# The first two blocks of a retention and FFN kernel: another order of v, q, k and g, x and weights loaded in one paced run, and tiles 4 to 7 transposed on TensorE

## The reference

```python
xn = _layernorm(x)
q1, k1 = apply_rotary(xn @ Wq, xn @ Wk)        # 4 heads of 256
v = xn @ Wv                                    # 4 heads of 512
...
    attn = einsum('bhid,bhjd->bhij', qb, kb) * D
    o_intra = einsum('bhij,bhjd->bhid', attn, vb)
    o_inter = einsum('bhid,bhde->bhie', qb * cross_q, S)
    S_new = gC * S + einsum('bhjd,bhje->bhde', kb * cross_k, vb)
...
s = (rmsnorm(o) * silu(xn @ Wg)) @ Wo
g = _silu(ffn(xn))                             # down(silu(gate) * up)
x = x + s * g
```

## Time and profile before

| | before |
|---|---|
| time, 3 runs | median 2100.38 us, 2098.61 to 2416.41 |
| profiled execution | 2097.79 us |
| its span on the slowest core | 2095.9 us (cores: 2090.8 to 2095.9) |
| TensorE busy | 2037.7 us, 97% of the span |
| VectorE, ScalarE, POOL busy | 697.3, 489.5, 360.2 us |
| granted TensorE clock, mean | 0.992 |
| chain that ended last | PE 94%, DMA 3%, DVE 1%, issue 1%, SPq 1% |

### The profile page before, as it was taken

How to read it: one execution, slowest core, us unless ns; L and a number is a source line. 1 busy time by engine, 2 the same in 40 slices (tenths; PEclk the granted TensorE clock), 3 DMA queues, 4 the chain that set the end, 5 groups by cost and what they waited for, 6 DMA issues and landing times.

```text
span 2095.9 us, 28365 instructions; the slowest of 8 cores (2090.8 to 2095.9 us)
## 1 busy us (share of the span) xinstructions
PE 2037.7 (97%) x9484; PEld 937.6 (45%) x9676; DVE 697.3 (33%) x1156; ACT 489.5 (23%) x880; POOL 360.2 (17%) x996
## 2 busy tenths in 40 slices
PE   5789999999999999999999999999999999999998
PEld 3334444444444444444444444444444444444443
DVE  4444445442232231132234454545311211211211
ACT  2333343442101101101013443343210110110110
POOL 1134444444100000000103333333300000000000
PEclk9899999999999999999999999999999999999999
DMA  7666888769645545545733334534772352452432
GB/s 166 134 93 108 113 122 138 140 122 221 188 115 176 146 109 179 155 118 170 140 75 58 64 65 73 86 67 88 169 216 71 121 171 71 140 151 71 152 90 70
DMA packets 221501, 257.80 MB, mean 123 GB/s; under 512 B 140336, under 2 KB 157872, under 8 KB 221360
## 3 DMA queue, kind: packets, MB, share of 16 engines
q1 hardware_dynamic: 191408, 201.44, 35.0%
q0 software_dynamic: 29952, 54.54, 19.0%
HBM read 244.39 MB, written 46.14 MB: 139 GB/s over the span
## 4 chain that ended last, share of the span: by engine, by line
PE 94%; DMA 3%; DVE 1%; issue 1%; SPq 1%; ACT 0%; POOL 0%; DVEq 0%; ACTq 0%; POOLq 0%
PE R L381 61%; PE U L697 16%; PE OA L716 11%; PE U L492 2%; PE OA L524 2%; PE OA L519 1%; DMA xa<-x 1%; DMA xnT<-xn 1%; PE R L471 1%; DMA wvA<-wv 1%; DMA ktok<-kT 0%; SPq L202 0%; SPq L198 0%; ACT xn L335 0%; DVE st L296 0%
## 5 line engine op out<-in xcount | busy, mean ns | idle before, releaser
L381 PE MATMUL R<-xnT,wgu 128*128 128x512 bf16 x3010 | 663.3, 379 | 3.3
L381 PEld LDWEIGHTS R<-xnT,wgu 128*128 128x128 bf16 x3072 | 300.4, 98 | 361.0
L697 PE MATMUL U<-wd_sb,hT 128*128 128x512 bf16 x1504 | 334.7, 379 | 1.6
L669 DVE TENSOR_TENSOR hT<-sg,R 128x512 bf16<-128x512 bf16 x192 | 131.9, 688 | 492.1 <-PE R L381 482.7
L660 ACT ACTIVATE sg<-R 128x512 bf16<-128x512 f32 x192 | 114.6, 597 | 568.3 <-PE R L381 545.9
L697 PEld LDWEIGHTS U<-wd_sb,hT 128*128 128x128 bf16 x1536 | 150.3, 98 | 181.2
L716 PE MATMUL OA<-wo_sb,ogl 128*128 128x512 bf16 x1006 | 225.3, 379 | 1.0
L504 DVE SCALAR_TENSOR_TENSOR S<-S,U 128x1024 bf16<-128x1024 bf16 x112 | 136.7, 1220 | 203.7 <-PE U L492 199.4
L724 DVE TENSOR_TENSOR g<-g,OA 128x1024 f32<-128x1024 f32 x32 | 39.1, 1222 | 430.8 <-PE OA L716 430.8
L716 PEld LDWEIGHTS OA<-wo_sb,ogl 128*128 128x128 bf16 x1024 | 100.2, 98 | 120.8
L708 ACT ACTIVATE g<-U 128x1024 f32<-128x1024 f32 x32 | 32.7, 1023 | 481.8 <-PE U L697 465.5
(11 more groups left out here) (87 smaller groups left out, 1639.6 us busy)
## 6 DMA issues: line engine op xcount, KB each, us to landing
wgu<-wgu_bf SPq DMA_DIRECT2D x192, 512.0 KB, 4.4
og_sp<-og SPq DMA_DIRECT2D x128, 128.0 KB, 4.0
ox<-x SPq DMA_DIRECT2D x32, 512.0 KB, 5.7
out<-ox SPq DMA_DIRECT2D x32, 512.0 KB, 3.1
wd_sb<-fdw POOLq DMA_DIRECT2D x48, 256.0 KB, 7.7
xa<-x SPq DMA_DIRECT2D x16, 512.0 KB, 9.5
xl<-x SPq DMA_DIRECT2D x16, 512.0 KB, 5.3
wgu_bf<-fgw POOLq DMA_DIRECT2D x24, 256.0 KB, 6.1
```

What stands on the lines that cost most here:

```text
L381: ins = e.matmul(ring[r][:, :], l, m, start=(k == 0), stop=(k == KC - 1))
L669: t_ev = DVE.do(lambda e: e.tensor_mul(out=hT[:, m * 512:(m + 1) * 512], in0=sg[:, g0:g0 + 512], in1=ring[r][:, :]), sDVE)
L697: ins = e.matmul(U[:, n * 512:(n + 1) * 512], hT[:, k * 512 + tt * 128:k * 512 + (tt + 1) * 128], wd_sb[:, k * D + n * 512:k * D + (n + 1) ...
```

## The change

Sequence 0 gets its groups in another order: for the first two blocks v of block 0, q and k of block 0, v of block 1, g of block 0, q and k of block 1, g of block 1. Blocks 2 and 3 keep theirs (two v, q and k, two v, g), and so do all others. `ret.slot(p - 12)` is unchanged and now goes by the running number p. Tiles 4 to 7 are transposed on TensorE, behind p = 7 (tiles 4 and 5) and p = 9 (6 and 7), with their applies and the chain of 6 and 7 placed among the groups of block 0. SP loads xa 0 to 7 and the first two rope tables in one run without a wait; POOL starts two pieces of wvA without a wait, the other two when xa 0 is there, wqA and wkA when xa 3 is, wgA when xa 5 is. xa 12 to 15 are loaded behind p = 9. The chain of tiles 8 to 11 moves forward to p = 16, that of 12 to 15 back by one group, and the applies from n = 7 and 9 to n = 8 and 10. The second `warm` has 24 matmuls and not 44.

```diff
-    def order(s, bi):
-        if s == 0 and bi < 2:
-            return (4, 5, 6, 7, 0, 1, 2, 3, 8, 9, 10, 11)
...
+    def order(s):
+        qk, v, g = (0, 1, 2, 3), (4, 5, 6, 7), (8, 9, 10, 11)
+        if s:
+            return [(bi, x) for bi in range(16) for x in qk + v + g]
+        first = [(0, v), (0, qk), (1, v), (0, g), (1, qk), (1, g)]
...
-    xa_load(2)
-    xa_load(3)
-    POOL.wait(xa_tok[0])
-    for a_ in w_pieces(0, 0):
+    for t in (2, 3, 4, 5):
+        xa_load(t)
+    cs_load(0)
+    for t in (6, 7):
+        xa_load(t)
+    cs_load(1)
+    for n, a_ in enumerate(w_pieces(0, 0)):
+        if n in (2, 4, 8):
+            POOL.wait(xa_tok[{2: 0, 4: 3, 8: 5}[n]])
         w_load(*a_)
...
-    warm(44)
-    ln0_pair(2, True)
-    SP.wait(w_tok[(0, 0, 2)])
-    cs_load(0)
-    for t in range(4, 8):
-        xa_load(t)
-    for t in (4, 6):
-        ln0_pair(t, False)
-        ln0_trans(t, ln_tok[t])
-        ln0_trans(t + 1, ln_tok[t + 1])
-    cs_load(1)
+    warm(24)
+    ln0_pair(2)
+    apply0(2, False)
+    apply0(3, True)
+    ln0_pair(4)
...
+    def ln0_step(p):
+        if p < 2:
+            ln_trans_pe(p + 2, ln_tok[p + 2])
+        elif p == 3:
+            apply0(4, True)
+            apply0(5, True)
+        elif p == 5:
+            ln0_pair(6)
+            apply0(6, False)
+        elif p == 7:
+            apply0(7, True)
+            ln_trans_pe(4, ln_tok[4])
+            ln_trans_pe(5, ln_tok[5])
+        elif p == 9:
+            ln_trans_pe(6, ln_tok[6])
+            ln_trans_pe(7, ln_tok[7])
+            for t in range(12, 16):
+                xa_load(t)
+        elif 12 <= p < 40:
+            t, n = 8 + 4 * (p // 12 - 1), p % 12
+            if p < 24 and n < 4 or p >= 24 and n in (0, 1, 4, 6):
+                ln0_stats(t + (n if p < 24 else (0, 1, 4, 6).index(n)))
+            elif n == (4 if p < 24 else 7):
+                ln_tok["c"] = ln0_chain(0, 4)
+            elif n in (8, 10):
+                for u in (t + n - 8, t + n - 7):
+                    apply0(u, True)
+                    ln0_trans(u, ln_tok[u])
```

More of the change, by code:

```diff
@@ L356, in ln_trans_pe @@
         t_pe = PE.do(tr, sPE)
-        xn0_free[t] = t_pe
+        xn0_free[t % 8] = t_pe
         ACT.wait(t_pe)
@@ L739, in warm, with ln0_pair, apply0 @@
             PE.do(lambda e: e.matmul(ring[3][:, 0:256], idm_sb[:, 0:128], idm_sb[:, :], start=True, stop=True))
-    def order(s, bi):
-        if s == 0 and bi < 2:
-            return (4, 5, 6, 7, 0, 1, 2, 3, 8, 9, 10, 11)
-        if s == 0 and bi < 4:
-            return (4, 5, 0, 1, 2, 3, 6, 7, 8, 9, 10, 11)
-        return range(12)
+    def order(s):
[3 more added lines that the diff above has]
+        first = [(0, v), (0, qk), (1, v), (0, g), (1, qk), (1, g)]
+        for bi in (2, 3):
+            first += [(bi, v[:2]), (bi, qk), (bi, v[2:]), (bi, g)]
+        first += [(bi, qk + v + g) for bi in range(4, 16)]
+        return [(bi, x) for bi, xs in first for x in xs]
     ln_tok = {}
-    def ln0_pair(t, act):
+    def ln0_pair(t):
         ln0_stats(t)
         ln0_stats(t + 1)
[L754 to L759, removed]
-    consts()
-    xa_load(2)
-    xa_load(3)
-    POOL.wait(xa_tok[0])
-    for a_ in w_pieces(0, 0):
+        ln_tok["c"] = ln0_chain(t % 4, 2)
+    def apply0(t, act):
+        ln_tok[t] = ln0_apply(t, ln_tok["c"], act)
+    for t in (0, 1):
+        xa_load(t)
+    consts()
+    for t in (2, 3, 4, 5):
[7 more added lines that the diff above has]
+            POOL.wait(xa_tok[{2: 0, 4: 3, 8: 5}[n]])
         w_load(*a_)
@@ L768, in build_nc @@
     warm(32)
-    ln0_pair(0, True)
+    ln0_pair(0)
+    apply0(0, False)
+    apply0(1, True)
     ln_trans_pe(0, ln_tok[0])
     ln_trans_pe(1, ln_tok[1])
-    warm(44)
-    ln0_pair(2, True)
-    SP.wait(w_tok[(0, 0, 2)])
-    cs_load(0)
-    for t in range(4, 8):
-        xa_load(t)
-    for t in (4, 6):
-        ln0_pair(t, False)
-        ln0_trans(t, ln_tok[t])
-        ln0_trans(t + 1, ln_tok[t + 1])
-    cs_load(1)
+    warm(24)
+    ln0_pair(2)
+    apply0(2, False)
+    apply0(3, True)
@@ L783, in build_nc @@
+    ln0_pair(4)
     for t in range(8, 12):
         xa_load(t)
+    cs_load(2)
+    cs_load(3)
     gn_load()
[L787 to L804, removed]
+    def ln0_step(p):
[15 more added lines that the diff above has]
+            for t in range(12, 16):
+                xa_load(t)
+        elif 12 <= p < 40:
[8 more added lines that the diff above has]
+                    ln0_trans(u, ln_tok[u])
@@ L806, in build_nc @@
     for s in range(SEQ):
         ret = Ret(s)
[L808 to L813, removed]
+        for p, (bi, g) in enumerate(order(s)):
+            ret.slot(p - 12)
+            proj(s, bi, g)
+            if s == 0:
+                ln0_step(p)
+            bi = p // 12
+            if p % 12 < 11:
+                continue
```

## The result

| | before | after |
|---|---|---|
| time, median of the undisturbed executions | 2099.5 us (2098.61 and 2100.38) | 2081.98 us (2081.22 to 2082.36) |
| ratio after to before | | 0.9916, 95% interval 0.9887 to 0.9945 |
| span of the slowest core in the profile | 2095.9 us (core 2) | 2080.4 us (core 5) |
| mean of the eight spans | 2093.3 us | 2074.9 us |

In some executions cores ran at a lower granted clock and up to some 20% longer, with either kernel; the times and ratios here leave those executions out, and of the profiles of e6 and e9, which were taken in such executions, only the cores that the table names are read.

What follows compares the result with a forecast made beforehand. TensorE was taken as the bound, busy 2037.7 of 2095.9 us, so only its waits counted. From 2097.8 us, 13 (A) and 12 (B) off gave 2072.8; with the median 2.6 above, 2075, range 2064 to 2088.

Steps and rivals of the forecast that it cites:

- the old waits: TensorE's waits before upd(0); three were to give way to one of about 6 us ahead of p = 8.
- the slower rival: p = 8 starts 8 us after xa 7 lands; with xa 7 from 60 us on the kernel is slower; chance 0.02.
- p = 0 to 7 ... takes 14.65 us, unchanged: First groups of block 0, with the transposes of tiles 2 and 3, were to take as long as before.
- a wait for wk: In block 0, 0 to 2 us possible, said to lie under the following wait, which does not depend on k.
- Two signs: Among the signs of being wrong: a wait for wgA or wkA over 2 us, and upd(0) after 58 us.
- I keep p = 0 at 20.6: Start of the first group: constants 1 to 3 us later, shorter warm giving about as much back; bounds 19 to 23.
- x and constants come late: At the start, a slip of 4 us delays p = 8 equally: 2079; a slip of 8: 2083; chance 0.15.
- A: Stretch from p = 0 to upd(0), 45.75 us before; 13 us gained, 7 to 16 with the bounds.
- B: Stretch from upd(0) to the upd behind p = 26, 46.4 us before; 12 us gained, ends 5 and 15.
- Stretch C: Block 3: the 2.90 us wait and a slow group stay; gain taken as nothing, -3 to +2.
- the transposes stay slow: Transposes of tiles 8 to 11 again take 12.5 us beside wqB pieces: 2082, with ktok slow too 2085; chance 0.22.
- the dearer cases: Slow transposes, 2080 to 2088, chance 0.22, and late x, 2078 to 2090, chance 0.15.

Runs made afterwards that it cites:

- e6: Changed kernel with tiles 4 to 7 transposed by DMAs from SP again, each behind its apply; no execution faster than 2091.2 us, no ratio.
- e9: Changed kernel with head 1's 12 weight pieces paced two each behind chunks 4, 5, 8, 9, 10 and 11 of sequence 0; 2080.0 us, ratio 0.9907.
- e2: Changed kernel with wqA and wkA issued directly behind wvA, without the wait for xa 3; 2083.3 us, ratio 0.9912.
- e3: Changed kernel with the first two pieces of wvA also held back until xa 0 is there; 2086.3 us, ratio 0.9926.
- e5: Changed kernel with head 1's weights paced from chunk 4 on in sequence 0, not from chunk 2; 2082.5 us, ratio 0.9912.
- e12: Changed kernel with stats, chain, applies and transposes of tiles 12 to 15 back in their old places, unused stats removed; 2084.8 us, no ratio.

## Why the prediction was right or wrong

*Right: what replaces the old waits.* Ropes, ktok and wgA no longer stop TensorE, but for 0.2 us on one core; one wait for L359 stands ahead of p = 8, of 5.6 us on core 5 and 3.4 on the mean, where 6 were forecast; from the rope of q to p = 8 it is 9.9 us against 10.2 on core 5, and from p = 0 in e2, where the weights are there, 22.5 against 22.3. The transposes cost 1.06 us for two tiles, near the 1.3 from the row. The range held, and no core shows 60 us at xa 7, the condition of the slower rival.

*Wrong, first: "p = 0 to 7 ... takes 14.65 us, unchanged".* On the mean of the cores it took 20.2 us, on core 5 21.0 (22.89 to 43.90). The forecast saw a wait for wk and called it covered, since the chain does not depend on k. But the same wait for xa 3 holds wqA, and the chain does depend on q: the rope started 14.2 us behind p = 0 on the mean, and not 12.1. The price is 2.0 us at p = 8 (e2 against the changed kernel, mean), of which 0.9 are left at upd(0). On core 5 the rope came 17.5 us behind p = 0: of the 5.4 more, 2.0 are the wait for wqA, 1.7 the two q groups behind it at low clock (5.30 and not 3.62), and about 1.6 the transposes of tile 2, which waited for a late x too.

The step fails in a second place: the chain does depend on k. The apply of tile 7 stands on ScalarE behind the cast of k's second half, and where wkA is late this cast ends after VectorE's chain. Core 1 of the changed kernel, rows of PE, of DVE (the end of the chain) and of ACT (the cast, the apply):

```profile
39.58 4.99 PE L381 MATMUL R<-xnT,wkA 128*128 128x512 bf16 x16 [4.00 <-DMA wkA<-wk]
...
43.76 0.16 DVE L321 SCALAR_TENSOR_TENSOR nl<-mv,nl 128x2 f32<-128x2 f32 x1
...
44.66 0.59 ACT L394 CAST eraw<-R 128x512 bf16<-128x512 f32 x1 [1.14 <-PE R L381]
45.15 1.24 ACT L335 ACTIVATE xn<-xa,nl 128x1024 bf16<-128x1024 f32 x1
```

The chain is through at 43.9, the apply starts at 45.15. So it is on cores 0, 1 and 3, by 0.5 to 1.2 us. Two signs that the prediction named for being wrong point here: wkA is waited for by more than 2 us on four cores (0, 1, 3 and 7, 2.8 to 4.0), and upd(0) comes after 58 on core 5.

The underlying slip is that no arrival time was worked out for xa 3. Before, the stats of tile 3 started at 14.3 us (mean) without a wait for x; now they wait for it until 19.4 (20.6 on core 5), because the two early pieces of wvA take their share of the DMA engines: in e3, which holds them back, it is 14.0 again.

*Wrong, second: "I keep p = 0 at 20.6".* It is 22.3 on the mean and 22.9 on the slowest core, within the stated bounds. Constants came 4 us later (13.2 against 9.1), not 1 to 3. The rival "x and constants come late" is this mechanism, through the constants and xa 3, and its size fits: it had A at 9 for a slip of 4 us, and p = 8 came at 46.8 against the forecast's 42.9, with 8.3 won in A. xa 7, which it also named, delayed nobody: the stats of tile 7 never waited for it.

*Wrong, third: B.* 12 us were forecast, 7.9 came on the mean (44.2 to 36.3). The mechanism, weight pieces beside transposes, was named, and e5 shows that it makes up 4.5 of the 4.9 us still lost there. The loss was put at 3 us.

*The choice of core.* The sum went by core 2, which was the slowest in that execution and above the mean in its marks: upd(0) at 66.3 against a mean of 64.8, B 46.4 against 44.2. On the means the stages give 8.3 + 7.9 + 1.7 = 17.9 us, close to the 18.4 by which the mean span fell from the one profiled execution to the other; over all undisturbed executions it fell by 16.0. By core the gain between the two profiles runs from 10.4 (core 5) to 23.5 us (core 0), but as the slowest core changes from execution to execution, this is scatter and belongs to no core. Of the 7 us between forecast and result nearly 4 are this choice (1.5 in A, 2.2 in B), some 3 the late start in A (1.7 at p = 0, 1.5 behind it), 2 the size in B; block 3 gives 1.7 back, where nothing was forecast.

*Stretch C* was forecast at nothing. The new places of stats, chain and applies together were not a cost but a gain of 1.8 us (e12).

*Luck.* The measured 2082 is also what the rival "the transposes stay slow" had, with 13 us won in A and 5 in B. That is chance: 8.3, 7.9 and 1.7 were won. The range held because it took in the dearer cases; A and B each lay 4 to 5 us under their forecasts, near the low end of their own bounds.

*A reading.* The forecast puts both waits of block 2 ahead of q groups. In the earlier trace rows the one of 2.40 us stands ahead of a v group.

## What to carry to other kernels

When loads are put in a new order, work out an arrival time for every tile that something is paced by, not only for those that TensorE reads; a wait on POOL for a tile is a new consumer of it, and what it holds back may lie ahead of the chain that ends last. Follow on each in-order engine not only what an instruction waits for but what stands ahead of it: the cast of k ahead of an apply, an apply ahead of a copy. Sum a program on eight cores over the mean of the cores, and compare kernels by it too, since the slowest core changes from one execution to the next. And when single edits each win a few microseconds in their stage and little in the time, try them together before they are dropped.
